# A delta-rule layer on one core: residuals from three half-width pieces, and more of the work on GpSimd

## The reference, cut to what matters

```python
x = x + L0_attn(xn) + L0_ffn(xn)               # first block, not touched
xn = layernorm(x)
qkv, z, b_raw, a_raw = xn @ W_qkv.T, xn @ W_z.T, xn @ W_b.T, xn @ W_a.T
conv = silu(sum(w[:, j] * padded[:, :, j:j + T] for j in range(4)))
q, kk, v = split(conv)                          # q, kk repeated for the two value heads, l2-normed
beta, decay = sigmoid(b_raw), exp(-exp(A_log) * softplus(a_raw + dt_bias))
def step(state, inp):                           # a scan over 256 positions
    state = state * d_t[..., None, None]
    Sk = einsum('bhi,bhij->bhj', k_t, state)
    delta = (v_t - Sk) * b_t[..., None]
    state = state + einsum('bhi,bhj->bhij', k_t, delta)
    o = einsum('bhi,bhij->bhj', q_t, state)
    return state, o
y = o * silu(z); y = y * rsqrt(mean(y * y) + 1e-06) * norm_w
attn = y @ W_out.T
h = square(relu(xn @ up_w)) @ down_w; f = h + (xn @ expert_weight) * sum(top2(xn @ gate_w))
x = x + attn + (f - mean(f)) * rsqrt(var(f) + 1e-05) * ln_gamma + ln_beta
```

## Time and profile before

| | |
|---|---|
| time, median of 3 runs | 1802.42 us (1801.4 to 1803.45) |
| the profiled execution, its own time | 1804.3 us |
| its span in the trace | 1802.3 us |
| PE busy | 1703.3 us (95%) |
| DVE, ACT, POOL busy | 1316.0 (73%), 1167.9 (65%), 652.5 us (36%) |

### The profile page before, as it was taken

One profiled execution on the slowest core, in us unless ns is written; L12 is line 12 of the kernel. 1 busy time (PEld: TensorE's weight loads), 2 busy tenths in 40 slices (PEclk: granted clock), 3 DMA queues, 4 the chain that ended last, 5 costly groups with the idle time before them and its releaser, 6 DMA issues.

```text
span 1802.3 us, 34261 instructions
## 1 busy us (share of the span) xinstructions
PE 1703.3 (95%) x13208; PEld 1322.5 (73%) x13208; DVE 1316.0 (73%) x2293; ACT 1167.9 (65%) x2185; POOL 652.5 (36%) x474
## 2 busy tenths in 40 slices
PE   7899999999998987999999999999999999999986
PEld 5676766767665666787787787877877877878875
DVE  7788888888866267767768767777677687677753
ACT  3335353443535465778878878887787788788762
POOL 2222213222214063615516426336246165163340
PEclk9999999999999997999999999999999999999998
DMA  3111010101103200110110101101101201111000
GB/s 138 35 55 47 33 67 33 67 33 55 46 1 105 76 19 1 37 59 25 37 56 28 36 25 60 36 25 37 59 25 36 60 25 36 38 47 36 7 2 24
DMA packets 51447, 75.16 MB, mean 42 GB/s; under 512 B 3392, under 2 KB 41792, under 8 KB 51312
## 3 DMA queue, kind: packets, MB, share of 16 engines
q1 hardware_dynamic: 51312, 73.28, 12.6%
HBM read 72.03 MB, written 1.25 MB: 41 GB/s over the span
## 4 chain that ended last, share of the span: by engine, by line
PE 54%; ACT 7%; DVE 6%; issue 3%; DVEq 0%
PE bank L731 12%; PE bank L911 7%; PE bank L751 5%; PE bank L866 4%; PE bank L789 3%; PE bank L802 2%; PE bank L816 2%; PE bank L812 2%; DVE d_sil L1334 2%; ACT d_dec L1133 2%; PE bank L874 2%; PE bank L887 2%; PE bank L854 2%; PE bank L888 2%; PE bank L889 2%
## 5 line engine op out<-in xcount | busy, mean ns | idle before, releaser
L1634 POOL TENSOR_TENSOR d_dec<-d_dec,d_qk 128x384 f32<-128x384 f32 x128 | 138.8, 1111 | 638.4 <-DVE d_N L1359 571.3
L1334 DVE SCALAR_TENSOR_TENSOR d_sil<-d_pre,d_w,d_sil 128x1024 f32<-128x1024 f32 x192 | 295.2, 1538 | 10.1 <-ACT d_pre L1099 9.9
L731 PE MATMUL bank<-xnT,d_w 128*128 128x512 f32 x480 | 242.4, 617 | 0.0
L189 PE MATMUL bank<-xnT,a_w 128*128 128x512 f32 x512 | 236.6, 596 | 0.0
L1380 DVE CAST_PREDICATED d_X<-tables_sb,bank 128x512 bf16<-128x512 int32 x192 | 134.3, 700 | 89.9 <-PE bank L802 76.4
L1396 DVE TENSOR_TENSOR d_Rb<-d_V,bank 128x512 bf16<-128x512 f32 x128 | 86.5, 685 | 109.8 <-PE bank L866 109.8
L489 POOL TENSOR_TENSOR a_hidc<-a_hid,a_comb 128x512 f32<-128x512 f32 x32 | 44.4, 1387 | 295.0 <-DVE a_hid L336 295.0
L189 PEld LDWEIGHTS bank<-xnT,a_w 128*128 128x128 f32 x512 | 90.6, 192 | 78.5 <-issue 78.5
L1161 ACT ACTIVATE d_T<-bank 128x512 bf16<-128x512 f32 x160 | 100.5, 628 | 65.2 <-PE bank L812 62.6
L866 PE MATMUL bank<-d_W,d_N 128*128 128x128 f32 x1024 | 130.6, 281 | 2.0 <-DVE d_W L1401 1.9
L508 ACT ACTIVATE a_sg<-a_sm 128x384 f32<-128x384 f32 x64 | 33.0, 515 | 152.0 <-DVE a_sm L341 152.0
(11 more groups left out here) (210 smaller groups left out, 4274.8 us busy)
## 6 DMA issues: line engine op xcount, KB each, us to landing
d_dec<-decay_scratch SPq DMA_DIRECT2D x32, 512.0 KB, 5.7
a_w<-w SPq DMA_DIRECT2D x16, 897.0 KB, 4.6
d_w<-w SPq DMA_DIRECT2D x16, 776.0 KB, 4.6
a_comb<-comb_scratch SPq DMA_DIRECT2D x16, 512.0 KB, 5.6
d_dec<-decay_scratch SPq DMA_DIRECT2D x32, 256.0 KB, 6.1
d_wo<-w SPq DMA_DIRECT2D x16, 256.0 KB, 3.1
f_w<-w SPq DMA_DIRECT2D x8, 256.0 KB, 4.2
x_sb<-x SPq DMA_DIRECT2D x2, 512.0 KB, 4.4
```

Source lines behind the costliest of these rows:

```text
L189: last = pe.matmul(psum[bank][:, :], wq(slot, part, k), xnT[:, k, half * HALF:(half + 1) * HALF], start=(k == 0), stop=(k == KT - 1))
L731: last = pe.matmul(psum[bank][:, :], cols(slot, (c * KT + k) * P, P), xnT[:, k, h * HALF:(h + 1) * HALF], start=(k == 0), stop=(k == KT - 1))
L1334: dve.scalar_tensor_tensor(sil[c][:, :, :], pre[c % 2][:, :, tap:tap + S], cols(slot, OC + 4 * c + tap, 1), sil[c][:, :, :], ALU.mult, ALU ...
L1634: pool.tensor_tensor(g, g, qk[b][:, :, :], ALU.mult).then_inc(s["p_done"], 1)
```

## The change

The matrix `N` is written as a sum of three bf16 pieces: `Nh` is `N` rounded (ScalarE, `high`), `Nm` is the rest rounded (GpSimd, `middle`: a subtraction and a copy), and `Nl` is what is then left (GpSimd, `lowest`, into the buffer of `Nb` once the inversion has read it). The solution is kept as terms: `W0b` from round 0 and `dWb` from round 1, both bf16. `residual` multiplies pieces with terms: two products in round 0, three more in round 1 which add to the same PSUM bank. `apply` no longer adds up. `Wv` is the sum of three terms: GpSimd adds `W0b` and `dWb` (`partial`), VectorE adds round 2's term from PSUM (`total`); `link` and `outputs` wait for that. The last convolution tile, `c` = 3, moves from VectorE to GpSimd, as a multiplication into a scratch buffer and an addition for each tap. The setting of the diagonal moves ahead of the scaling of `V`. The feed-forward's `f_y` moves to the buffers `yT`, its parts are spread over head 0, and `f_tail` works on halves of 1024 columns. The filling on PE, ACT and DVE is dealt out anew.

```diff
             def apply(i, v, c, a):
...
-                                     start=(a == 0 and b == 0), stop=(a == 2), skip_group_check=True)
+                                     start=True, stop=True)
             def residual(i, v, c, a):
                 if a == 0:
                     pe.wait_ge(s["w0_done"], i * 4 + 2 * c + v + 1)
-                    pe.wait_ge(s["diag_done"], i * 2 + v + 1)
+                    pe.wait_ge(s["nm_done"], i * 2 + v + 1)
+                    parts = ((Nh, W0b), (Nm, W0b))
                 else:
-                    pe.wait_ge(s[f"wup_done{v}"], i * 4 + 2 * c + a)
-                for b in range(B):
-                    last = pe.matmul(psum[5 + 2 * v][:, b * P:(b + 1) * P], N[v][:, b, 2 * c, :], Wv[v][:, b, c, :],
-                                     start=True, stop=True)
+                    pe.wait_ge(s["nl_done"], i * 2 + v + 1)
+                    pe.wait_ge(s[f"dw_done{v}"], i * 2 + c + 1)
+                    parts = ((Nl, W0b), (Nh, dWb), (Nm, dWb))
+                for n, (coef, vec) in enumerate(parts):
+                    for b in range(B):
+                        last = pe.matmul(psum[5 + 2 * v][:, b * P:(b + 1) * P], coef[v][:, b, c, :], vec[v][:, b, :],
+                                         start=(a == 0 and n == 0 and b == 0), stop=(a == 1 and n == 2), skip_group_check=True)
...
+            def high(i, v):                                    # ScalarE, fill[4][v]
+                act.wait_ge(s["diag_done"], i * 2 + v + 1)
+                act.activation(Nh[v][:, :, :, :], N[v][:, :, 0:3:2, :], ACT.Copy).then_inc(s["nh_done"], 1)
...
+                change(i, 0)                                   # ScalarE's solve
                 if nxt:
+                    conv_in(ns, ni, 3, (1,))
                     square(ni, 0)
+                    square(ni, 1)
+                for v in range(2):
+                    round_r2(i, v)
+                for v in range(2):
+                    first_w(i, v, 1)
+                if nxt:
                     batch_decays(ni, ns, 0)
+                change(i, 1)
...
+            def total(i, v, c):                                # VectorE
+                dve.wait_ge(s["apply_ready"], i * 12 + 6 * c + 4 + v + 1)
+                dve.wait_ge(s["wsum_done"], i * 4 + 2 * c + v + 1)
+                dve.tensor_tensor(Wv[v][:, :, c, :], Wv[v][:, :, c, :], psum[4 + 2 * v][:, :].rearrange("p (b d) -> p b d", b=B),
+                                  ALU.add).then_inc(s[f"wup_done{v}"], 1)
...
+            def conv(slot, i, c, steps):                       # GpSimd
+                part = N[0][:, :, 0:3:2, :]
+                for n in steps:
+                    tap = 2 - n
...
+                    pool.tensor_scalar(part, shifted, cols(slot, OC + 4 * c + tap, 1), None, ALU.mult).then_inc(s["tap_done"], 1)
+                    pool.wait_ge(s["tap_done"], (i - 1) * 3 + n + 1)
+                    f = sil[c][:, :, :].rearrange("p b (c t) -> p b c t", c=2)
+                    pool.tensor_tensor(f, f, part, ALU.add).then_inc(s["conv_step"], 1)
+            def middle(i, v):
+                pool.wait_ge(s["nh_done"], i * 2 + v + 1)
+                rest = N[v][:, :, 0:3:2, :]
+                pool.tensor_tensor(rest, rest, Nh[v][:, :, :, :], ALU.subtract).then_inc(s["mid_done"], 1)
+                pool.wait_ge(s["mid_done"], i * 2 + v + 1)
+                pool.tensor_copy(Nm[v][:, :, :, :], rest).then_inc(s["nm_done"], 1)
+            def lowest(i, v):
+                pool.wait_ge(s["nm_done"], i * 2 + v + 1)
+                pool.wait_ge(s["x_ready"], i * 12 + 2 * len(LEVELS) - 2 + v + 1)
+                pool.tensor_tensor(Nl[v][:, :, :, :], N[v][:, :, 0:3:2, :], Nm[v][:, :, :, :],
+                                   ALU.subtract).then_inc(s["nl_done"], 1)
+            def partial(i, v, c):
+                pool.wait_ge(s["w0_done"], i * 4 + 2 * c + v + 1)
+                pool.wait_ge(s[f"dw_done{v}"], i * 2 + c + 1)
+                pool.tensor_tensor(Wv[v][:, :, c, :], W0b[v][:, :, :], dWb[v][:, :, :], ALU.add).then_inc(s["wsum_done"], 1)
...
                 for v in range(2):                             # GpSimd's body, after V and Rb
+                    middle(i, v)
+                for v in range(2):
+                    lowest(i, v)
                 if nxt:
-                    mask(*nxt)
+                    for v in range(2):
+                        mask(*nxt, v)
+                for v in range(2):
+                    partial(i, v, 0)
+                if nxt:
+                    conv(nxt[1], nxt[2], 3, (0, 1))
+                for v in range(2):
+                    partial(i, v, 1)
+                if nxt:
+                    conv(nxt[1], nxt[2], 3, (2,))
```

More of the change, by code:

```diff
@@ L620, in layer1_phase @@
             gain = e.sb("f_gain", [P, NT])
-        f_y = y
+        f_y = [yT[v][:, :].rearrange("p (t d) -> p t d", d=D) for v in range(2)]
         UNITS = 8
@@ L631, in layer1_phase @@
         Wv = [m.sb(f"d_W{v}", [P, B, 2, P]) for v in range(2)]
+        Nh = [m.sb(f"d_Nh{v}", [P, B, 2, P], BF16) for v in range(2)]
+        Nm = [m.sb(f"d_Nm{v}", [P, B, 2, P], BF16) for v in range(2)]
+        Nl = Nb
+        W0b = [m.sb(f"d_W0b{v}", [P, B, P], BF16) for v in range(2)]
+        dWb = [m.sb(f"d_dWb{v}", [P, B, P], BF16) for v in range(2)]
         ysq = [Wv[v][:, :, :, :].rearrange("p b c d -> p (b c) d") for v in range(2)]
@@ L933, in body @@
                         fill[li][half].append(lambda n=n: project_out(*before, n, nxt))
-                ahead, between, behind, closing = ([[] for _ in range(6)] for _ in range(4))
+                between, inner, closing = ([[] for _ in range(6)] for _ in range(3))
                 if nxt:
@@ L950, in body @@
                     z = lambda n, half: (lambda: project_z(nxt[1], nxt[2], n, (half,)))
-                    ahead[0], between[0], behind[0] = [part(3, 1, 0)], [part(3, 1, 1)], [z(0, 0)]
-                    between[1], behind[1] = [z(0, 1)], [q(0, 0)]
-                    between[2], behind[2], closing[2] = [q(0, 1)], [q(1, 0)], [q(1, 1)]
-                    between[3] = [z(1, 0)]
-                    between[4] = [z(1, 1)]
+                    between[0], inner[0] = [part(3, 1, 0)], [part(3, 1, 1)]
+                    between[1] = [z(0, 0)]
+                    between[2], inner[2], closing[2] = [z(0, 1)], [q(0, 0)], [q(0, 1)]
+                    between[3], inner[3] = [q(1, 0)], [q(1, 1)]
+                    between[4] = [z(1, 0)]
+                    between[5] = [z(1, 1)]
                 invert(i, fill, after_turn)
@@ L959, in body @@
                         k = 3 * c + a
-                        for f in ahead[k]:
-                            f()
                         apply(i, 0, c, a)
@@ L965, in body @@
                         apply(i, 1, c, a)
-                        for f in behind[k]:
-                            f()
                         for v in range(2):
@@ L972, in body @@
                                 link(i, v)
+                            if v == 0:
+                                for f in inner[k]:
+                                    f()
                         for f in closing[k]:
@@ L1219, in body @@
                 key_norm(i)
-                if not first:
+                if first:
+                    act.wait_ge(ev["f_var"], 1)
+                    act.activation(f_std[:, :], f_std[:, :], ACT.Sqrt).then_inc(ev["f_std"], 1)
+                else:
                     root_y(i - 1)
@@ L1234, in body @@
                 invert(i, fill, [lambda: conv_in(ns, ni, 0, (0,))] if nxt else ())
-                if first:
-                    act.wait_ge(ev["f_var"], 1)
-                    act.activation(f_std[:, :], f_std[:, :], ACT.Sqrt).then_inc(ev["f_std"], 1)
                 for v in range(2):
@@ L1412, in add_out @@
                 need(dve, s["acc_done"], (i - 1) * 4 + n + 1)
+                if i == 0 and n == 0:
+                    dve.wait_ge(ev["added"], 2)
                 a = acc[:, 2 * n:2 * n + 2, :]
@@ L1466, in body @@
                 first = isinstance(i, int) and i == 0
-                if not first:
+                if first:
+                    f_moments()
+                else:
                     sum_y(i - 1, 0)
@@ L1504, in body @@
                         k = 3 * c + a
-                        if first and k == 1:
-                            f_scale()
-                        if a:
-                            update(i, c, a)
+                        if a == 1:
+                            change(i, c)
+                        elif a == 2:
+                            for v in range(2):
+                                total(i, v, c)
                         for f in mid[k]:
@@ L1634, in decayed, with diagonal @@
                     pool.tensor_tensor(g, g, qk[b][:, :, :], ALU.mult).then_inc(s["p_done"], 1)
+            def diagonal(i, v):
+                pool.wait_ge(s["nb_done"], i * 2 + v + 1)
```

(13 more changed lines are left out.)

125 lines of the change are left out of this document (62 added, 63 removed).

## The result

| | before | after |
|---|---|---|
| median of the runs, us | 1802.41 | 1862.95 (1861.54 to 1864.35, 4 runs) |
| ratio, 95% interval | 1 | 1.0336 [1.0318, 1.0354], slower |
| span of the profiled execution | 1802.3 | 1859.8 |
| start of head 0 | 641.6 | 638.3 |
| head 0 | 85.9 | 75.1 |

The account below looks back on a forecast made before the run. PE's own work bounds the kernel before; afterwards GpSimd's chain to the link decides. 14 heads x 3.4 = 48, less 4 for the ends, gives +44 us: 1848 by the profiled clock, 1846 against the median; range 1787 to 1882.

Parts of the forecast that it names:

- PE's gain: Residuals and apply blocks on PE: shorter bf16 work saves 2.7 us a head, at most some 4.5 us.
- GpSimd's chain: GpSimd from `high` through `middle`, `lowest`, masks and `partial`: link starts at 1204.1 without contention, 1206.3 with it.
- the contention: Shared port of VectorE and GpSimd: three convolution steps delay the chain 0 to 3.6 us, taken as 2.2.
- the slow rival: GpSimd's mixed-type operations take 2.8 us each, all three steps in the way: +6.8 us a head, 1893; chance 13%.
- the first rival: GpSimd keeps up, bf16 operands at 1.90 us or below: link at 1202.0, -0.9 us a head, 1785; chance 22%.
- Behind the link: PE from the link's start to the head's end: 17.6 us, against 15.9 before.
- The price of `tensor_scalar`: One-input operation on GpSimd, 1024 columns: 1.04 us, at worst 1.9; roughly line rate would be about 0.85.
- no throughput bound: GpSimd's total work: 26.8 us added to 31.2 makes 58 us a head, which fits in a head.
- The ends: Head 0 with its tail into head 1 about 0, last head wins 3 to 4 us: -4, with 8 either way.
- The head's own late link: Head 0's link, late as in other heads, takes back 3.4 of some 8 us of waiting saved.
- The last head: Without masks or filling, it wins 3 to 4 us from shorter products.
- the likeliest case: Forecast's own case, full or half contention on GpSimd's chain: +2 to +5 us a head, 1825 to 1869; chance 50%.

Follow-up runs that it names:

- the kernel with both edits: Against the changed kernel, GpSimd's masks moved behind the first partial sum and the last convolution tile put back on VectorE; 1761.25 us, 0.9771 of the kernel before.

## Why the prediction came out as it did

**PE's gain: right.** 2.7 us a head were forecast; without the long waits, in the kernel with both edits, PE's busy time was 2.54 less.

**GpSimd's chain: right, within 2 us.** Put on the clock of the forecast (20.26 us earlier), `high` is there at 1185.3 (forecast 1185.05) and the link starts at 1204.6 (forecast 1206.3). PE arrives at 1200.5 (forecast 1200.2) and waits 4.12 us. From `high` to the end of the first `partial` it was 18.6 us where I had 20.4: the mixed subtractions take 2.13, not 2.37 (four of them with `lowest`, 1.0 us in all), the masks and `partial` 0.3 less, and the contention costs 1.8 (the two copies take 1.91 and 1.99 where 1.04 is the shortest, in the last head, without steps beside them) and not 2.2. Mixed types cost nothing (2.13 against 2.36 for single precision throughout), so the slow rival is out; that they save only so little keeps the first rival out as well, since the link would have had to start at 1202.9.

**Behind the link: the term that was too small.** I had 17.6 us from the link to the next head; it took 20.53. The four groups at the clock of 0.52 took 6.56 instead of 3.61, 2.9 us. The rest, 13.97, is what was forecast (14.0), with 0.91 of waiting for `change` against 1.3. I priced work behind a wait at the duration it has in a head without one, although I forecast a wait of 5 to 6 us. Per head: 3.4 forecast, less 1.7 for the earlier link, plus 2.9 for the clock, 4.6; measured 4.66. Three experiments show the clock's share: 2.9 us with the masks early and 2.7 with PE kept busy, both from the link to the next head, and with the norms ahead up to 4.1 us between heads of one and the same kernel.

**The price of `tensor_scalar`: wrong by a factor.** 1.04 us was taken from the copy, 1.9 as the worst; it takes 2.85 with a factor from a column. A tap is 5.2 us, not 3.4. The 0.85 us that the prediction worked out beside it as an estimate is further off still. The tap was not on the first chain, as said, but it is what made the second `partial` late as soon as the first was mended, and what pushed head 1's tail back. The text had GpSimd as "no throughput bound", which holds (61.3 us of a head of 75.1), but the place before `outputs` was never laid out for GpSimd, only for ScalarE's copy.

**Contention.** The Trainium skill (SBUF — State Buffer, Who interferes with whom) calls the ports an exclusive lock, and the prediction took from it that all three VectorE steps would count in full, 20 us above my sum. The traces agree with the lock, but not with that count: what decides is which of the two instructions starts first. On the chain of a middle head two steps started first, 0.31 and 0.19 us ahead of GpSimd's copies; each step kept its 1.3 us and each copy took 0.9 more, 1.8 in all. The third step ends 0.2 us behind the first subtraction's start. Where a subtraction started first, it kept its 2.13 us and the step beside it took 2.64 instead of 1.28 (head 1, at 755.07 and 755.64); where a subtraction started behind a step, it was the longer one, 2.84 us (with the tile on VectorE, at 748.69). The masks moved early show the cost when many steps are beside them, 7.92 for 4.94.

**The ends: the sum was near, the parts were not.** Head 0 won 10.8 us; 4.6 was forecast (8 less 3.4). The 8 were right: in head 0 of the kernel before, PE waits 1.86, 3.60 and 2.87 us in its solve of chunk 0, 8.3 in all, beside the three long steps, and these waits are gone. The experiment with the short tail shows that they came from the tail. The head's own late link did not come: PE waits 13.3 us in its inversion, which has no output projection to fill it, reaches the link 57.5 us after the head's start, and finds `partial` done. Head 1 lost 11.1 where I had 3.4 + 5: 4.7 as every head and 6.4 from the tail, whose six operations now end at 727.7. GpSimd's `scale_y` comes late behind it, and PE waits at 739.21:

```profile
739.21 1.67 PE L909 MATMUL bank<-tables_sb,x_sb 128*128 128x128 f32 x8 [2.49 <-POOL x_sb L1669]
```

The last head shows no gain in these two traces, where 3 to 4 us were forecast. From the first `apply` to `outputs` it takes 16.9 us against 17.7, and so it does in every other trace with the pieces and without them: with no filling between the rounds it is bound by the hand-overs between the engines (PE waits for `d_Rb`, `d_dWb` and `d_W` a dozen times), not by PE's products. The 0.9 us won there can't be told from other differences: this end, with the same instructions in it, took 88.7, 86.8 and 89.9 us in the three kernels without the pieces and 85.7 to 90.4 in those with them. The start of head 0 at 638.3 against 641.6 is not the change's: the kernel before with a short tail has 638.45 as well, and the one with the tile moved 641.37. In the two that start late the granted clock was 0.52 from 527.9 to 535.0, in this kernel and the one with the short tail 1.00. What makes it differ stays open.

The range held, and the likeliest case was the right one. The mechanism carried the forecast; a price of 2.9 us a head was missing, and 1.7 too much stood in its place. That the two errors have opposite signs is luck. The 17 us between 1846 and 1863 add up so: 1.26 us too little in each of 14 heads, 17.6; the ends, -7.7 us and not -4, take 3.7 back; and some 3 come from the two profiled executions, which lie 1.9 above and 1.4 below their medians.
